# An expert stage's first row with a written order: group 0's routing in one go, six gelus ahead of the gates, left-over attention at named units

## The reference

```python
# attention (residual added outside)
q = jax.nn.softmax(q, axis=-2) * SCALE
k = jax.nn.softmax(k, axis=-1)
context = jnp.einsum('bhdn,bhen->bhde', k, v)
out = jnp.einsum('bhde,bhdn->bhen', context, q)
out = rmsnorm(out @ w_out + b_out, g_out)
# experts, on xn = layernorm(h) * gamma + beta
logits = jnp.einsum('bsd,de->bse', xn, Wr) + br
top_vals, top_idx = jax.lax.top_k(logits, K)          # K = 2 of E = 8
w = jax.nn.softmax(top_vals, axis=-1)
w_full = jnp.einsum('bsk,bske->bse', w, jax.nn.one_hot(top_idx, E))
for e in range(E):
    h = gelu(jnp.einsum('bsd,dh->bsh', xn, W1[e]) + b1[e])
    y = y + (h @ W2[e] + b2[e]) * w_full[..., e, None]
```

## Time and profile before

| | |
|---|---|
| median of 3 runs | 423.93 us |
| profiled execution | 424.18 us |
| its span, first to last instruction | 422.4 us |
| mean granted TensorE clock | 0.982 |
| first spread of the gates (start of the expert loop) | 320.25 us |
| last expert product | 417.79 us |
| busy share PE, DVE, ACT, POOL | 93%, 83%, 77%, 62% |

### The profile page before, as it was taken

One profiled execution on the slowest core, in us unless ns is written; L12 is line 12 of the kernel. 1 busy time (PEld: TensorE's weight loads), 2 busy tenths in 40 slices (PEclk: granted clock), 3 DMA queues, 4 the chain that ended last, 5 costly groups with the idle time before them and its releaser, 6 DMA issues.

```text
span 422.4 us, 6309 instructions
## 1 busy us (share of the span) xinstructions
PE 394.1 (93%) x1989; PEld 318.0 (75%) x1989; DVE 352.6 (83%) x851; ACT 326.1 (77%) x558; POOL 262.2 (62%) x388
## 2 busy tenths in 40 slices
PE   5798889999999999999999989999987998999995
PEld 2586578888888888888888878787766775876883
DVE  4887688888898889888889888999875888899885
ACT  1263689999999999888977854678846898988994
POOL 0575787778777779778776556685322654435452
PEclk9999999999999999999999998999996998999999
DMA  6800012122312321221112000000000000000001
GB/s 217 334 2 0 2 26 46 31 51 51 50 27 50 51 53 27 50 50 50 44 32 51 1 0 2 2 2 2 0 2 0 0 2 12 15 12 12 14 13 26
DMA packets 15849, 14.94 MB, mean 35 GB/s; under 512 B 9796, under 2 KB 10568, under 8 KB 15560
## 3 DMA queue, kind: packets, MB, share of 16 engines
q1 hardware_dynamic: 15816, 14.54, 13.8%
HBM read 13.42 MB, written 1.11 MB: 34 GB/s over the span
## 4 chain that ended last, share of the span: by engine, by line
PE 64%; DVE 18%; ACT 12%; issue 4%; DMA 1%; POOL 1%; SPq 0%; DVEq 0%; ACTq 0%
PE ps L1430 56%; PE ps L1453 4%; ACT hid L861 4%; ACT w_all L867 3%; ACT ezf L796 2%; DVE hid L1372 2%; DVE hh L1224 2%; DVE stats L941 1%; DVE x L1372 1%; PE ps L1461 1%; DVE st L1074 1%; DVE kstat L1164 1%; DMA xn<-in_w_f 1%; DVE xn_lo L1379 1%; DVE qmax L1176 1%
## 5 line engine op out<-in xcount | busy, mean ns | idle before, releaser
L675 ACT ACTIVATE hid<-ps,b_fold 128x512 f32<-128x512 f32 x128 | 84.0, 681 | 21.3 <-PE ps L1430 20.8
L1015 DVE TENSOR_TENSOR hid_lo<-hid,hid_hi 128x1024 fp32r<-128x1024 f32 x64 | 78.8, 1231 | 25.3 <-ACT hid_hi L680 25.1
L1430 PE MATMUL ps<-xn_hi,w_all 128*128 128x512 f32 x256 | 87.4, 402 | 0.6 <-DVE xn_lo L1010 0.6
L1430 PE MATMUL ps<-hid_hi,w_all 128*128 128x512 f32 x256 | 85.0, 393 | 0.0
L680 ACT ACTIVATE hid_hi<-hid 128x1024 fp32r<-128x1024 f32 x64 | 67.9, 1061 | 2.0
L1430 PEld LDWEIGHTS ps<-xn_hi,w_all 128*128 128x128 f32 x256 | 48.4, 189 | 10.8 <-issue 0.9
L1430 PEld LDWEIGHTS ps<-hid_hi,w_all 128*128 128x128 f32 x256 | 48.1, 188 | 9.9
L1430 PE MATMUL ps<-xn_lo,w_all 128*128 128x512 f32 x128 | 49.9, 390 | 0.0
L1430 PE MATMUL ps<-hid_lo,w_all 128*128 128x512 f32 x128 | 49.8, 389 | 0.0
L861 ACT ACTIVATE hid<-ps,eb_fold 128x512 f32<-128x512 f32 x64 | 44.1, 689 | 1.4 <-PE ps L1430 1.2
L1430 PE MATMUL ps<-hid_hi,ew 128*128 128x512 f32 x128 | 43.1, 421 | 1.9 <-ACT hid L861 1.8
(11 more groups left out here) (222 smaller groups left out, 898.2 us busy)
## 6 DMA issues: line engine op xcount, KB each, us to landing
rstd_row<-roots SPq DMA_DIRECT2D x29, 256.0 KB, 3.8
hh<-in_tokens SPq DMA_DIRECT2D x8, 256.0 KB, 7.9
hid<-in_w SPq DMA_DIRECT2D x1, 1024.0 KB, 7.1
rstd_row<-in_w SPq DMA_DIRECT2D x1, 1024.0 KB, 10.2
out<-hh SPq DMA_DIRECT2D x7, 128.0 KB, 2.0
ew_raw<-in_expert_w SPq DMA_DIRECT2D x1, 512.0 KB, 9.7
roots<-rstd SPq DMA_DIRECT2D x29, 2.0 KB, 1.4
ew_raw<-in_expert_w SPq DMA_DIRECT2D x1, 256.0 KB, 9.9
```

Of the source, the lines that this page charges most:

```text
L675: act.activation(hid[:, j % 2, f, :], bank[f], ACT.Gelu, bias=b1_fold[:, j // B * F + f:j // B * F + f + 1]).then_inc(gelu_done, 1)
L1015: dve.tensor_tensor(hid_lo[:, j % 2, 2 * p:2 * p + 2, :], hid[:, j % 2, 2 * p:2 * p + 2, :], hid_hi[:, j % 2, 2 * p:2 * p + 2, :].bitcast( ...
L1430: return pe.matmul(out, lhsT, rhs, start=start, stop=stop)
```

## The change

On PE, ACT, DVE and POOL lap -1 is taken out of the common loop and written out as a list of its own, and the common rules for left-over work in the expert loop become a list of named units.

- **DVE:** all of group 0's routing stands in one block behind lap -2, with only `output_sums(5)` inside it. `softmaxes(7)` and `masked_context(7)` follow the block; `expert_z_lo(4)`, `scaled_output(5)`, `scaled_m(7)` and `residual_moments(5)` move into units 1 to 3. Rows 6 and 7 get other units.
- **ACT:** the load of the gelu table moves ahead of `output_squares(5)`, and six gelus (`LEAD = 6`) are put ahead of `copy_gates(0)`. In the loop iteration n takes gelu n + 6. The gelu slots grow from 4 to 8 (`NHG`), four of them in `x`.
- **PE:** `logits(0)` is followed by `hidden(0)` to `hidden(5)` among what is left of lap -1, and iteration n of the loop takes `hidden(n + 6)`. `keep_clock(7)` is gone. `projected_context(7)`, `expert_z_transposes(4)` and `attend(6)` move into units 0, 2 and 4.
- **Banks:** the hidden layer's two banks swap order, and row 4's transposes go to bank 1 instead of 6.

```diff
-            for m in range(FIRST_LAP, 0):
+            for m in range(FIRST_LAP, -1):
...
+            act.preload_act_table(ACT.Gelu)
+            output_squares(5, 1)
+            gelu(0)
+            k_turned(7, 1)
+            q_turned(6, 0)
+            gelu(1)
+            gelu(2)
+            ez_of(4, 0)
+            ez_hi(4, 0)
+            gelu(3)
+            gelu(4)
+            gate(0)
+            gelu(5)
+            copy_gates(0)
...
-                if n < UNITS:
-                    gelu(n)
+                if n + LEAD < UNITS:
+                    gelu(n + LEAD)
                 if 1 <= n <= UNITS:
                     hidden_hi(n - 1)
...
+                if n == 7:
+                    ez_of(5, 1)
+                if n == E:
+                    ez_hi(5, 1)
+                    output_squares(7, 1)
...
+            take_logits(0)
+            v = first_max(0)
+            v = first_hot(0, v)
+            output_sums(5, 1)
+            v = second_max(0, v)
+            v = second_hot(0, v)
+            v = weights(0, v)
+            gates_out(0, v)
+            v_total[7] = softmaxes(7, 1)
+            masked_context(7, 1)
...
+                if n == 1:
+                    expert_z_lo(4, 0)
+                if n == 2:
+                    scaled_output(5, 1)
+                if n == 3:
+                    scaled_m(7, 1, v_total[7])
+                    residual_moments(5, 1)
+                if n == 7:
+                    output_sums(6, 0)
+                if n == E:
+                    expert_z_lo(5, 1)
+                if n == E + 1:
+                    scaled_output(6, 0)
+                if n == E + 2:
+                    residual_moments(6, 0)
+                    output_sums(7, 1)
+                if n == E + 5:
+                    scaled_output(7, 1)
+                if n == E + 6:
+                    residual_moments(7, 1)
+                if n == E + 7:
+                    expert_z_lo(6, 0)
+                if n == 2 * E + 5:
+                    expert_z_lo(7, 1)
                 if m in (1, 3):
                     p = (m + 1) // 2
-                    if u == 2:
+                    if u == 4:
                         take_logits(p)
-                    if u == 3:
+                    if u == 5:
                         v = first_max(p)
...
+            logits(0)
+            pe.wait_ge(late_weights, 4)
+            hidden(0)
+            k_transposes(7, 1)
+            q_transposes(6, 0)
+            pe.wait_ge(kt_ready, B)
+            hidden(1)
+            context(7, 1)
+            for n in range(2, LEAD):
+                hidden(n)
+            pe.wait_ge(qsub_ready, B)
+            turn_gates(0)
...
-                if 2 <= n < UNITS:
-                    hidden(n)
+                if n + LEAD < UNITS:
+                    hidden(n + LEAD)
```

More of the change, by code:

```diff
@@ L45 @@
 SKEW = 4
+LEAD = 6
 REPEATS = 3
@@ L51 @@
 HEAD_BANK = (7, 6)
[L52 removed]
+HIDDEN_BANK = (4, 0)
 EARLY_HEADS = 5
@@ L867, in hidden_hi @@
                 act.activation(hw_hi[:, slot * S:(slot + 1) * S], hw(slot), ACT.Copy).then_inc(hwhi_act, 1)
+            z_turned(0, 0)
+            z_hi(1, 1)
+            act.preload_act_table(ACT.Exp)
+            z_turned(1, 1)
+            for m in range(FIRST_LAP, -1):
+                a, c, d, e, f = m + 9, m + 8, m + 7, m + 6, m + 5
+                if e >= 0:
+                    output_squares(e, e % 2)
+                if c >= 0:
+                    k_turned(c, c % 2)
+                if d >= 0:
+                    q_turned(d, d % 2)
+                if f >= 0:
+                    ez_of(f, f % 2)
+                    ez_hi(f, f % 2)
+                exp_k(a, a % 2)
+                if a + 2 < B:
+                    z_hi(a + 2, a % 2)
+                if 0 < a and a + 1 < B:
+                    z_turned(a + 1, (a + 1) % 2)
+                copy_v(a, a % 2)
+                if f >= 0:
+                    expert_z_turned(f)
+                exp_q(a, a % 2)
@@ L869, in _ @@
+            act.preload_act_table(ACT.Gelu)
[12 more added lines that the diff above has]
+            copy_gates(0)
             for n in range(UNITS + SKEW + 2):
                 m, u = divmod(n, E)
-                if u == 4 and m + 5 < B:
-                    ez_of(m + 5, (m + 5) % 2)
@@ new lines, in _ @@
+                if n == 6:
+                    output_squares(6, 0)
+                if n == 7:
[4 more added lines that the diff above has]
+                if n == E + 2:
+                    expert_z_turned(5)
+                if n == E + 6:
+                    ez_of(6, 0)
+                if n == E + 7:
+                    ez_hi(6, 0)
+                if n == 2 * E + 2:
+                    expert_z_turned(6)
@@ L887, in _ @@
+                if n == 2 * E + 3:
+                    ez_of(7, 1)
+                if n == 2 * E + 4:
+                    ez_hi(7, 1)
+                if n == 2 * E + 7:
+                    expert_z_turned(7)
                 if u == 3 and m in (2, 4):
@@ L1382, in output @@
-            def output(b):
-                for k, part in enumerate(parts_of_row(b)):
-                    t = slice(part.start // P, part.stop // P)
-                    halves, row = tiles(sum_bank(b, k), P)[:, t, :], tiles(h1[:, b, :])[:, t, :]
-                    dve.wait_ge(yt_done, b + k + 1)
-                    v = own.inc(dve.tensor_tensor(row, halves[:, :, 0:D2], row, ALU.add))
-                    own.wait(v)
-                    dve.tensor_tensor(row, halves[:, :, D2:P], row, ALU.add).then_inc(out_ready, 1)
+            take_logits(0)
@@ L1418, in _ @@
                         gates_out(p, v)
-                if u == 6 and m + 6 < B:
-                    scaled_output(m + 6, m % 2)
-                if u == 5 and m + 5 < B:
-                    expert_z_lo(m + 5, (m + 5) % 2)
                 if 1 <= n <= UNITS and lo_by_dve(n - 1):
@@ L1860, in _ @@
                     q_transposes(7, 1)
+                    projected_context(7, 1)
+                if n == 2:
+                    expert_z_transposes(4, 0)
+                if n == 4:
+                    attend(6, 0)
                 if SKEW <= n < UNITS + SKEW:
@@ L1866, in _ @@
                     attend(7, 1)
-                if u == 7 and m + 5 < B:
-                    expert_z_transposes(m + 5, (m + 5) % 2)
-                if u == 2 and m in (1, 3):
+                if n == E + 1:
+                    expert_z_transposes(5, 1)
+                if n == 2 * E + 1:
+                    expert_z_transposes(6, 0)
+                if n == 2 * E + 6:
+                    expert_z_transposes(7, 1)
+                if u == 3 and m in (1, 3):
                     logits((m + 1) // 2)
```

136 lines of the change are left out of this document (43 added, 93 removed).

## The result

The changed kernel takes 431.22 us in the median of four runs (430.88 to 432.32), the kernel before 424.01 us in four runs beside it (423.75 to 424.59). The ratio is 1.019, with a 95% interval of 1.0164 to 1.0217: slower, by 7.2 us. The prediction was 418.4 us, and the range ended at 422.8.

The account below looks back on a forecast made before the run. No engine was idle for long, so waits between engines were taken as the bound; terms -1.4 + 0.7 - 0.85 - 1.75 - 0.9 - 1.3 = -5.5 us from 424.18 gave 418.7, predicted median 418.4, range 413.8 to 422.8.

Parts of the forecast that it names:

- rival 1: Expert layernorm hand-offs ACT-DVE-PE arrive late, also for rows 6 and 7, with lower clock: costs 6.7, about 425.3 us; chance 0.09.
- The gates: Stretch from group 0's logits to the first spread: spread at 318.9 instead of 320.25, limited by ACT's tanh; -1.4 us.
- Row 0: First expert row: takes over work that stood before it, mostly covered by DVE's idle time; 12.6 instead of 11.88, +0.7 us.
- Row 1: Second expert row: DVE's 12.5 us of work sets it, products no longer wait for gelus; 12.8 instead of 13.65, -0.85 us.
- Row 2: Third expert row: six gelus of lead remove a wait, DVE's list becomes the limit; 13.2 instead of 14.95, -1.75 us.
- Rows 3 to 6: Middle expert rows: half of the 1.8 us over PE's own time in rows 3 to 5 goes, row 6 stays; -0.9 us.
- Row 7: Last expert row: the lead is paid out, no hidden layers or gelus left in it; 8.1 instead of 9.43, -1.3 us.
- The tail: Stretch behind row 7: claimed to stay at 7.86 us.
- The table load: ACT's gelu table load, moved earlier: costs nothing; a skill rule's drain of about 1.38 us would make the sum -4.8.

Follow-up runs that it names:

- Late routing alone: Kernel before with only the logits, `take_logits` and `first_max` of groups 1 and 2 moved to the change's later iterations; 428.16 us, ratio 1.0107.
- the best version: Changed kernel with gates earlier, hand-off distances restored, row 6's norm ahead of row 7's, row 7's `ez_of` one iteration earlier, `expert_z_lo` one later; 420.68 us, ratio 0.9941.

## Why the prediction was wrong, step by step

*The method.* My walk of the lists counted which data each step needs. It left out `wait_turned()`, the hand-off of a bank, so that five of the six waits had no term at all, and it took a step's iteration as its place in time. The iteration numbers that the diff gives for ACT, DVE and PE were in the prediction's reach, and the table of distances above can be made from them and the lists before. The one hand-off that I did walk (rival 1: row 5's `ez_hi`, `expert_z_lo`, transposes) I put at 1.5 us on DVE and as much on PE. DVE's wait measured 1.42, PE's 2.03, because `expert_z_lo(5)` itself took 1.28 us. Rival 1 was right in kind and in sign: stops at the turning steps, the lower clock behind one of them. It had 0.09, since I saw one place of six; that its 425.3 lies nearer to the result than the forecast is no credit, for it put the same wait at rows 6 and 7, and at row 7 the releaser is another and at row 6 there is none.

*The gates* (-1.4, measured 0.0). The walk from `hidden(0)` to the first spread was 11.7 us. In the run with `take_logits` ahead, whose ACT and PE lists are the change's up to there, it measures 317.50 - 305.93 = 11.57, with the tanh 8.34 behind `hidden(0)` (8.4 predicted). In the changed kernel's own profile it is 320.24 - 307.08 = 13.16. Its timelines, DVE's wait for the tanh and the last steps on PE:

```profile
316.55 0.21 ACT L821 ACTIVATE top<-top 128x16 f32<-128x16 f32 x1
...
316.87 0.29 DVE L1334 TENSOR_TENSOR scratch<-scratch,top 128x128 f32<-128x128 f32 x1 [4.60 <-ACT top L821]
...
318.37 1.09 PE L1783 MATMUL ps<-cons,w_all 128*128 128x128 f32 x4 [1.50 <-issue]
```

The tanh behind five gelus was the limit and DVE stood idle for it (3 us predicted, 4.60 measured), as the prediction had it. The missing 1.3 us go with PE at the lower clock from 308 to 311 us, below.

*Row 0* (+0.7, measured +2.8). The work that it took over was counted, the stop of `turn_gates(1)` was not. With that stop and row 4's steps out of the row it took 12.93 us; 12.6 was predicted with those steps in it. *Row 1* (-0.85, measured +3.45) is the term that failed most: the stops of 2.03 and 1.21 us and the lower clock behind the second. I said that the 1.5 us of the walked hand-off were in the sum, but 12.8 us for the row leave 0.3 us over the 12.5 of DVE's work, so they were not. DVE's work itself was sized well (11.99 us busy). Late routing alone made the same 17.1 us in the kernel before. *Row 2* (-1.75, measured +0.1): six gelus of lead were to take the wait for `second_max` away, and DVE's 12.9 us of work to be the limit. DVE was busy 14.14 us there, which by itself rules out 13.2. And PE writes `hidden(n + 6)` into one of two banks, and must wait for `gelu(n + 4)` of ACT's iteration n - 2, as before. The lead frees DVE from ACT, not PE. The lead alone in the kernel before agrees: no gain, and PE's wait there 1.83 us against 1.81. In the change itself that wait is down to 0.51 us (at 361.52), and the stops of 0.72 and 1.56 us stand in its place. *Rows 3 to 6* (-0.9, measured +1.4): all of it in row 3, where `turn_gates(4)` waits for group 2's logits; late routing alone gave row 3 2.6 us.

*Row 7* (-1.3, measured -1.25) was right, since no turning step is left there. The tail grew by 0.25.

*The table load.* ACT's timeline of the changed kernel:

```profile
305.49 1.28 ACT L869 ACT_TABLE_LOAD   x1
306.78 0.38 ACT L796 ACTIVATE osq<-ps 128x256 f32<-128x256 f32 x1
```

The next instruction starts 0.01 us behind the load, as in the earlier trace rows. The Trainium skill (ScalarE: Activation LUTs, "What ACT_TABLE_LOAD costs") would have had a drain there; the trace shows none.

*What stays open.* Row 0 and row 1 of the best version are still 1.4 and 1.5 us longer than before. For row 1 the trace names row 7's output on POOL, with `ez_hi(6)` close behind it; for row 0 I tried nothing further. Row 0 of before ran at a granted clock of 0.78 and took 11.88 us; with all places moved but no lead it ran at 1.00 and took 10.09, so the best version's 13.26 at 1.00 is further off than the 1.4 says. The loss of 7.2 us is taken apart between stops and clock only by the estimate above, from one profile of each kernel.

## What to carry to other kernels

When steps of several engines share a buffer, write for each of them the iteration of its reader beside the iteration of its next writer, before and after a move, and do the same for each input and its user. A distance that shrinks can be a new wait on the engine that writes, and what it feeds can stop with it; here six distances shrank, five of a shared bank and one of an input, and in place of a forecast gain of 5.5 us there was a loss of 7.2. Moving a chain means moving every link of it: with four engines in it, mending one end left the wait at another.
